# A three-product float32 gated expert layer: P1 copied into P2's bank and summed there by TensorE, the second prefix added into P5's bank

## The chip, the cores and the metric

The kernel runs on one core of one Trainium2 chip. The metric is the device time of one launch in microseconds (us); lower is better. Engines are named as in the profile: PE (TensorE's matmuls), PEld (its weight loads), DVE (VectorE), ACT (ScalarE), POOL (GpSimd), SP (SyncE, which issues the DMAs).

## The reference

```python
def _L0_cond_ref(h, gating_probs, shared_gate_prob, Wg, Wu, Wd, Sg, Su, Sd):   # h: 16 x 256 tokens x 256
    g = jnp.einsum('bsd,edf->ebsf', h, Wg)                                       # 8 experts, f = 1024
    u = jnp.einsum('bsd,edf->ebsf', h, Wu)
    expert_outs = jnp.einsum('ebsf,efd->ebsd', jax.nn.silu(g) * u, Wd)
    expert_output = jnp.einsum('be,ebsd->bsd', gating_probs, expert_outs)
    shared = jnp.einsum('bsf,fd->bsd', jax.nn.silu(h @ Sg) * (h @ Su), Sd)
    sg = shared_gate_prob[:, :, None]
    return (1.0 - sg) * expert_output + sg * shared
x = x + _L0_cond_ref(x, ...)
```

All of it is float32. The shared weights are a ninth expert whose coefficient is the shared gate.

## The kernel before

**Tiling.** The 4096 tokens are 8 tiles of 512 columns, taken in 4 groups of two (t = 0 and 1). For each group the kernel goes through 9 experts, and in each through 8 chunks of 128 of the 1024 inner features. One (group, expert, chunk) is a *unit*, numbered n; there are 4 x 9 x 8 = 288. Expert 0 of a group is written out; experts 1 to 8 are a hardware loop of 8 units, so there are 32 loop iterations.

**A unit.** Gate and up of one chunk for both tiles are a 2 x 2 by 2 x 2 block product, made Strassen-Winograd fashion from seven 128 x 128 by 128 x 512 products P1 to P7 instead of eight, plus four products into the down projection (two for each tile). Each product is three matmuls (`product`): a number is split in a high part (hi, rounded to fp32r) and a rest (lo), and hi·hi, hi·lo and lo·hi are summed. That is 11 products or 33 matmuls in a unit. The prefix sums are U2 = P1 + P6 and U3 = U2 + P7, kept in the bank `chain_ps` (two of them, by the parity of n); then gate of tile 0 = P1 + P2, gate of tile 1 = U2 + P5 + P3, up of tile 1 = U3 + P5, and up of tile 0 = U3 + P4.

**What the engines do in a unit.** PE issues P4 of the unit before (P4(n-1)), then P1, P5, the two down products of tile 0 for unit n-2, P6, P2, P3, P7, and the two down products of tile 1 for unit n-1. ACT copies P1 and P5 and, after P6, U2 to SBUF ("taps", L411, L414, L421), applies Silu twice (L429, L432), makes the hi parts of h of both tiles (L395 for tile 1, L400 for tile 0) and the hi part of the weights of unit n+2 in two casts (L374). DVE makes gate0 = tap of P1 + P2 (L516), gate1 = tap of U2 + (P5 + P3) (L522), up1 = tap of P5 + U3 (L528, into the bank of P2), then h1 = silu x coefficient x up1 in place (L493, two halves), the lo of h1 (L508), h0 in place in the chain's bank (L482, two halves) and the lo of h0 (L501). POOL makes the sums and the lo parts of the weights and of x. The trace joins names that differ in a digit: `p_up_ps` is the bank `p2_up1_ps`, `p_ps` is `p53_ps`, `tap_p` is tap_p1 or tap_p5, `h_hi` is h0_hi or h1_hi.

**What sets the order.** It is written out by hand. Every engine executes its own queue in order, and engines wait for each other through semaphores (`wait_ge`); `after(engine, signal, count)` is such a wait that is left out in the first units. The units are software-pipelined: ACT's and DVE's unit n begins with the second half of the work on unit n-1:

```python
h1_hi_of(n - 1)      # ACT, then the tap of P1(n), the tap of P5(n), h0_hi_of(n - 1), the weights' first cast
...
h1_lo_of(n - 1)      # DVE, then h0, h0_lo_of(n - 1), gate0(n), gate1(n), up_of_1(n), h1(n)
```

In the first six units of groups 0 to 2 ACT also casts forms of the next group's x (`x_form_hi`, L390; one in each of five units, two in the sixth), between the second weight cast and the first Silu. In the first two units of groups 1 to 3 DVE adds the down banks of the group before into `acc` (L534), behind h1.

Of the kernel before, what the change touches and what calls it, by code (L numbers as in the profile page):

```python
# [25 lines left out]
def moe_kernel(nc, xT, w, probs, shared_gate, out):  # L26
# [12 lines left out]
    with ExitStack() as ctx:  # L39
# [229 lines left out]
        def _(pe):  # L269
# [16 lines left out]
            def down0(k, start, stop, each=False):  # L286
                for c in range(DC):
                    last = product(
                        down_ps[:, 0, c, :], k % SLOTS, D0 + c, h0_hi[:, k % 2, :], h0_lo[:, k % 2, :], start, stop
                    )  # L290
                    if each and c == 0:
                        last.then_inc(down_done[0], 1)
                last.then_inc(down_done[0], 1)

            def down1(k, start, stop):
                for c in range(DC):
                    last = product(down_ps[:, 1, c, :], k % SLOTS, D0 + c, h1_hi[:], h1_lo[:], start, stop)
                last.then_inc(down_done[1], 1)
# [9 lines left out]
            def unit(g, e, k):  # L308
# [37 lines left out]
                if not isinstance(n, int) or n > 0:  # L346
                    pe.wait_ge(h_lo_done[1], n)
                    opens = in_first and k == 1
                    if opens:
                        after(pe, added[1], g)  # L350
                    down1((k - 1) % CHUNKS, start=opens, stop=first)
# [334 lines left out]
```

## Time and profile before

| | |
|---|---|
| median of 3 runs | 2179.14 us (2177.81 to 2179.55) |
| the profiled execution's own time | 2178.35 us |
| its span, from the first to the last instruction | 2176.5 us |
| granted TensorE clock, mean | 1.000 |
| PE busy | 2159.4 us, 9504 matmuls |
| DVE busy | 1490.3 us, 2623 instructions |
| ACT busy | 1532.3 us, 2623 instructions |
| POOL busy | 1386.7 us, 2046 instructions |

A profile's page gives busy times, groups of instructions with the idle time ahead of them and who ended it, and the chain of work that ended last; the timeline lists instructions by start. One matmul shows as 0.39 us long, but they overlap: the next one starts before the first has ended. An ACT or DVE instruction, too, may start before the end of the one before it on its engine.

### The profile page before, as it was taken

What the parts mean: (1) busy time and instruction counts of PE and PEld (TensorE: products, weight loads), DVE (VectorE), ACT (ScalarE), POOL (GpSimd) and SP (SyncE); (2) the same over time, 40 slices, a digit from 0 to 9 for tenths busy, and PEclk for the clock granted to TensorE, in tenths of its full rate; (3) what the DMA queues carried; (4) which work ended last, traced back from release to release, by engine and by line L of the source; (5) the groups of instructions that cost most, each with busy time, mean ns of one, the idle gap of its engine ahead of it and who ended that gap; (6) DMA issues with size and microseconds to landing.
All of it is one profiled execution on the core that took longest, in us unless ns stands there. A gap on an engine that the chain in (4) does not pass through costs nothing.

```text
span 2176.5 us, 34574 instructions
## 1 busy us (share of the span) xinstructions
PE 2159.4 (99%) x9504; PEld 1785.0 (82%) x9504; DVE 1490.3 (68%) x2623; ACT 1532.3 (70%) x2623; POOL 1386.7 (64%) x2046
## 2 busy tenths in 40 slices
PE   7999999999999999999999999999999999999999
PEld 5888888888888888888888888888888888888887
DVE  6666666666766666666676666666667666666666
ACT  7767776776777677767777776777677677767775
POOL 7766666666866666666686666666666666666663
PEclk9999999999999999999999999999999999999999
DMA  4111111111211111111121111111112111111110
GB/s 151 59 51 56 52 51 51 58 51 51 72 57 51 51 57 51 51 51 58 51 71 54 55 51 51 58 51 51 51 58 70 52 54 54 51 51 58 51 51 27
DMA packets 44683, 122.22 MB, mean 56 GB/s; under 512 B 5088, under 2 KB 5344, under 8 KB 44640
## 3 DMA queue, kind: packets, MB, share of 16 engines
q1 hardware_dynamic: 44640, 121.73, 18.0%
q8 instruction: 17, 0.28, 0.1%
q14 instruction: 26, 0.21, 0.0%
HBM read 117.51 MB, written 4.19 MB: 56 GB/s over the span
## 4 chain that ended last, share of the span: by engine, by line
PE 99%; DMA 0%; SPq 0%; POOL 0%; DVE 0%; ACT 0%; issue 0%; DVEq 0%; ACTq 0%
PE chain_ps L274 12%; PE down_ps L274 12%; PE down_ps L275 12%; PE down_ps L276 12%; PE chain_ps L275 12%; PE chain_ps L276 12%; PE p_ps L275 6%; PE p_ps L274 6%; PE p_ps L276 6%; PE p_up_ps L275 3%; PE p_up_ps L274 3%; PE p_up_ps L276 3%; DMA acc<-xT 0%; POOL w_lo L205 0%; SPq L145 0%
## 5 line engine op out<-in xcount | busy, mean ns | idle before, releaser
L205 POOL TENSOR_TENSOR w_lo<-w_raw,w_hi 128x384 fp32r<-128x384 f32 x861 | 850.8, 1019 | 731.5 <-ACT w_hi L374 731.5
L190 POOL TENSOR_TENSOR w_raw<-w_raw 128x128 f32<-128x128 f32 x1148 | 506.9, 464 | 32.6 <-DMA w_raw<-w 10.1
L274 PE MATMUL chain_ps<-x_hi,w_hi 128*128 128x512 f32 x1152 | 449.4, 390 | 11.7 <-DVE w_lo L590 5.8
L275 PE MATMUL chain_ps<-x_lo,w_hi 128*128 128x512 f32 x1152 | 448.6, 389 | 0.0
L276 PE MATMUL chain_ps<-x_hi,w_lo 128*128 128x512 f32 x1152 | 448.6, 389 | 0.0
L274 PE MATMUL down_ps<-h_hi,w_hi 128*128 128x512 f32 x1152 | 448.2, 389 | 0.2 <-DVE h_lo L508 0.2
L275 PE MATMUL down_ps<-h_lo,w_hi 128*128 128x512 f32 x1152 | 448.1, 389 | 0.0
L276 PE MATMUL down_ps<-h_hi,w_lo 128*128 128x512 f32 x1152 | 448.1, 389 | 0.0
L374 ACT CAST w_hi<-w_raw 128x768 fp32r<-128x768 f32 (+1 forms) x574 | 387.3, 675 | 85.1 <-PE down_ps L276 78.8
L395 ACT CAST h_hi<-p_up_ps 128x512 fp32r<-128x512 f32 x288 | 169.0, 587 | 307.8 <-DVE p_up_ps L493 307.8
L516 DVE TENSOR_TENSOR gate<-tap_p,p_up_ps 128x512 f32<-128x512 f32 x288 | 198.0, 687 | 251.0 <-PE p_up_ps L276 251.0
L501 DVE TENSOR_TENSOR h_lo<-chain_ps,h_hi 128x512 fp32r<-128x512 f32 x288 | 199.2, 692 | 200.8 <-ACT h_hi L400 175.5
L508 DVE TENSOR_TENSOR h_lo<-p_up_ps,h_hi 128x512 fp32r<-128x512 f32 x288 | 199.3, 692 | 188.7 <-ACT h_hi L395 188.7
L493 DVE SCALAR_TENSOR_TENSOR p_up_ps<-silu,coef,p_up_ps 128x256 f32<-128x256 f32 x576 | 253.7, 487 | 36.2 <-DVE p_up_ps L528 7.9
L274 PEld LDWEIGHTS chain_ps<-x_hi,w_hi 128*128 128x128 f32 x1152 | 216.4, 188 | 58.9 <-DVE w_lo L590 5.8
L274 PEld LDWEIGHTS down_ps<-h_hi,w_hi 128*128 128x128 f32 x1152 | 216.2, 188 | 45.6 <-DVE h_lo L508 0.6
L276 PEld LDWEIGHTS chain_ps<-x_hi,w_lo 128*128 128x128 f32 x1152 | 216.5, 188 | 45.0
L275 PEld LDWEIGHTS chain_ps<-x_lo,w_hi 128*128 128x128 f32 x1152 | 216.5, 188 | 44.6
L276 PEld LDWEIGHTS down_ps<-h_hi,w_lo 128*128 128x128 f32 x1152 | 216.2, 188 | 44.9
L275 PEld LDWEIGHTS down_ps<-h_lo,w_hi 128*128 128x128 f32 x1152 | 216.2, 188 | 44.8
L482 DVE SCALAR_TENSOR_TENSOR chain_ps<-silu,coef,chain_ps 128x256 f32<-128x256 f32 x576 | 251.1, 482 | 0.4 <-PE chain_ps L276 0.4
L411 ACT COPY tap_p<-chain_ps 128x512 f32<-128x512 f32 x288 | 169.6, 589 | 111.1 <-PE chain_ps L276 111.0
(47 smaller groups left out, 2852.6 us busy)
## 6 DMA issues: line engine op xcount, KB each, us to landing
w_raw<-w SPq DMA_DIRECT2D x287, 384.0 KB, 3.0
outT<-acc SPq DMA_DIRECT2D x7, 512.0 KB, 4.4
acc<-xT SPq DMA_DIRECT2D x6, 512.0 KB, 9.4
acc<-xT SPq DMA_DIRECT2D x4, 256.0 KB, 4.7
outT<-acc SPq DMA_DIRECT2D x2, 256.0 KB, 2.8
w_raw<-w SPq DMA_DIRECT2D x1, 256.0 KB, 3.0
w_raw<-w SPq DMA_DIRECT2D x1, 128.0 KB, 5.2
probs_sb<-probs SPq DMA_DIRECT2D x1, 64.0 KB, 7.7
```

The source lines that it names most:

```text
L190: nc.gpsimd.tensor_tensor(raw[:, cols(dst, dst)], raw[:, cols(a, a)], raw[:, cols(b, b)], op).then_inc(w_sums, 1)
L205: ins = nc.gpsimd.tensor_tensor(w_lo[:, s, c], w_raw[:, s, c], w_hi[:, s, c].bitcast(F32), ALU.subtract)
L274: nc.tensor.matmul(bank, w_hi[:, s, c], hi, start=start, stop=False, **on)
L275: nc.tensor.matmul(bank, w_hi[:, s, c], lo, start=False, stop=False, **on)
L276: return nc.tensor.matmul(bank, w_lo[:, s, c], hi, start=False, stop=stop, **on)
L374: nc.scalar.copy(w_hi[:, s, c], w_raw[:, s, c]).then_inc(w_hi_done, 1)
L411: nc.scalar.copy(tap_p1[:], chain_ps[:, k % 2, :]).then_inc(p1_tapped, 1)
L482: ins = nc.vector.scalar_tensor_tensor(sums, silu[:, 0, s], coef_of(g, e, 0, half), sums, ALU.mult, ALU.mult)
L493: ins = nc.vector.scalar_tensor_tensor(p2_up1_ps[:, s], silu[:, 1, s], coef_of(g, e, 1, half), p2_up1_ps[:, s], ALU.mult, ALU.mult)
L501: nc.vector.tensor_tensor(h0_lo[:, k % 2], chain_ps[:, k % 2, :], h0_hi[:, k % 2].bitcast(F32), ALU.subtract).then_inc(h_lo_done[0], 1)
L508: nc.vector.tensor_tensor(h1_lo[:], p2_up1_ps[:], h1_hi[:].bitcast(F32), ALU.subtract).then_inc(h_lo_done[1], 1)
L516: nc.vector.tensor_tensor(gate[:, 0], tap_p1[:], p2_up1_ps[:], ALU.add).then_inc(gate0_done, 1)
```

## The change

DVE's two gate additions become one addition of another kind, and of ACT's three copies to SBUF one goes and one goes to PSUM:

- P1 is copied by ACT (the *seed*) not to SBUF but into the bank that P2 will go to, now called `y_ps`, and P2 is accumulated on top of it by PE. gate0 is then in the bank without an addition. One matmul at the start opens the bank.
- U4 = tap of P5 + U2 is added by DVE (`u4`) into P5's own bank, now called `z_ps`, and P3 is accumulated on top. gate1 is then in that bank. The tap of U2 is gone.
- Both Silus read a PSUM bank.
- PE's order becomes P4(n-1), P1, P5, first down product of tile 0, P6, second down product of tile 0, P2, P7, P3, and the two of tile 1. P6 waits for the seed, P7 for u4.
- The seed waits for the lo of h1 of the unit before (`h_lo_done[1]`), since it overwrites h1's bank. It is ahead of the cast of h0 on ACT, as the tap of P1 was; the lo of h1 is ahead of h0 on DVE, as before.
- On ACT the second weight cast and x's forms now stand behind the first Silu and ahead of the second.

```diff
-        tap_p1 = sb("tap_p1", [P, TOKENS])
...
-        tap_u2 = sb("tap_u2", [P, TOKENS])
-        gate = sb("gate", [P, 2, TOKENS])
...
                 if opening:
                     first_w(0)
+                    nc.tensor.matmul(y_ps[:], w_hi[:, 0, 0:P], x_of(0, B11, True)[0], start=True, stop=True).then_inc(
+                        y_opened, 1
+                    )
...
-                after(pe, gate1_done, n)
+                after(pe, silu_done[1], n)
...
-                pe.wait_ge(p1_tapped, n + 1)
+                product(z_ps[:], s, S1, *x_of(g, T1, first), start=True, stop=True).then_inc(p5_done, 1)
+                down0_part(0)
+                pe.wait_ge(p1_seeded, n + 1)
                 product(chain, s, S2, *x_of(g, T2, first), start=False, stop=True, goes_on=True).then_inc(p6_done, 1)
-                after(pe, h_lo_done[1], n)
-                product(p2_up1_ps[:], s, A12, *x_of(g, B21, first), start=True, stop=True).then_inc(p2_done, 1)
-                pe.wait_ge(p5_tapped, n + 1)
-                product(p53_ps[:], s, S4, *x_of(g, B22, first), start=False, stop=True, goes_on=True).then_inc(p3_done, 1)
-                pe.wait_ge(u2_tapped, n + 1)
+                down0_part(1)
+                product(y_ps[:], s, A12, *x_of(g, B21, first), start=False, stop=True, goes_on=True).then_inc(p2_done, 1)
+                pe.wait_ge(u4_done, n + 1)
...
                 product(chain, s, S3, *x_of(g, T3, first), start=False, stop=True, goes_on=True).then_inc(p7_done, 1)
...
+                product(z_ps[:], s, S4, *x_of(g, B22, first), start=False, stop=True, goes_on=True).then_inc(p3_done, 1)
+                down1_both()
...
                 act.wait_ge(p1_done, n + 1)
-                after(act, gate0_done, n)
-                nc.scalar.copy(tap_p1[:], chain_ps[:, k % 2, :]).then_inc(p1_tapped, 1)
+                if first:
+                    act.wait_ge(y_opened, 1)
+                after(act, h_lo_done[1], n)
+                nc.scalar.copy(y_ps[:], chain_ps[:, k % 2, :]).then_inc(p1_seeded, 1)
...
-                act.wait_ge(p6_done, n + 1)
-                after(act, gate1_done, n)
-                nc.scalar.copy(tap_u2[:], chain_ps[:, k % 2, :]).then_inc(u2_tapped, 1)
+                act.wait_ge(p2_done, n + 1)
+                after(act, h0_done, n)
+                nc.scalar.activation(silu[:, 0], y_ps[:], ACT.Silu).then_inc(silu_done[0], 1)
                 if ahead:
                     weight_hi(n + AHEAD, (k + AHEAD) % SLOTS, 1)
...
-                nc.scalar.activation(silu[:, 1], gate[:, 1], ACT.Silu).then_inc(silu_done[1], 1)
+                nc.scalar.activation(silu[:, 1], z_ps[:], ACT.Silu).then_inc(silu_done[1], 1)
...
+            def u4(n, k):
+                dve.wait_ge(p6_done, n + 1)
+                dve.wait_ge(p5_tapped, n + 1)
+                nc.vector.tensor_tensor(z_ps[:], tap_p5[:], chain_ps[:, k % 2, :], ALU.add).then_inc(u4_done, 1)
...
-                gate0(n)
-                gate1(n)
+                u4(n, k)
                 up_of_1(n, k)
```

On PE, the first matmul of every product of one steady unit, before; `p53_ps` is P5's and P3's bank, `p2_up1_ps` P2's:

```order
L274 MATMUL chain_ps<-x_hi,w_hi 128x512 [waits h0_lo_done,w_lo_done]
...
L274 MATMUL p53_ps<-x_hi,w_hi 128x512 [waits gate1_done]
...
L274 MATMUL down_ps<-h0_hi,w_hi 128x512 [waits h0_lo_done]
...
L274 MATMUL down_ps<-h0_hi,w_hi 128x512
...
L274 MATMUL chain_ps<-x_hi,w_hi 128x512 [waits p1_tapped]
...
L274 MATMUL p2_up1_ps<-x_hi,w_hi 128x512 [waits h1_lo_done]
...
L274 MATMUL p53_ps<-x_hi,w_hi 128x512 [waits p5_tapped]
...
L274 MATMUL chain_ps<-x_hi,w_hi 128x512 [waits u2_tapped]
```

and now; `gate0_up1_ps` is `y_ps`, `p5_gate1_ps` is `z_ps`:

```order
L270 MATMUL chain_ps<-x_hi,w_hi 128x512 [waits h0_lo_done,w_lo_done]
...
L270 MATMUL p5_gate1_ps<-x_hi,w_hi 128x512 [waits silu1_done]
...
L270 MATMUL down_ps<-h0_hi,w_hi 128x512 [waits h0_lo_done]
...
L270 MATMUL chain_ps<-x_hi,w_hi 128x512 [waits p1_seeded]
...
L270 MATMUL down_ps<-h0_hi,w_hi 128x512
...
L270 MATMUL gate0_up1_ps<-x_hi,w_hi 128x512
...
L270 MATMUL chain_ps<-x_hi,w_hi 128x512 [waits u4_done]
...
L270 MATMUL p5_gate1_ps<-x_hi,w_hi 128x512
```

P6 stands one product earlier, and P7, which waits for DVE's u4, stands one product earlier and ahead of P3.

On ACT, one steady unit before, from the cast of h1 to the second Silu:

```order
L395 CAST h1_hi<-p2_up1_ps 128x512 [waits down1_done,h1_done]
L411 COPY tap_p1<-chain_ps 128x512 [waits gate0_done,p1_done]
L414 COPY tap_p5<-p53_ps 128x512 [waits up1_done,p5_done]
L400 CAST h0_hi<-chain_ps 128x512 [waits down0_done,h0_done]
L374 CAST w_hi<-w_raw 128x768 [waits down0_done,w_sums]
L421 COPY tap_u2<-chain_ps 128x512 [waits gate1_done,p6_done]
L374 CAST w_hi<-w_raw 128x384 [waits down0_done,w_sums]
L429 ACTIVATE silu<-gate 128x512 [waits h0_done,gate0_done]
L432 ACTIVATE silu<-gate 128x512 [waits h1_done,gate1_done]
```

and now:

```order
L402 CAST h1_hi<-gate0_up1_ps 128x512 [waits down1_done,h1_done]
L420 COPY gate0_up1_ps<-chain_ps 128x512 [waits h1_lo_done,p1_done]
L423 COPY tap_p5<-p5_gate1_ps 128x512 [waits up1_done,p5_done]
L407 CAST h0_hi<-chain_ps 128x512 [waits down0_done,h0_done]
L381 CAST w_hi<-w_raw 128x768 [waits down0_done,w_sums]
L430 ACTIVATE silu<-gate0_up1_ps 128x512 [waits h0_done,p2_done]
L381 CAST w_hi<-w_raw 128x384 [waits down0_done,w_sums]
L438 ACTIVATE silu<-p5_gate1_ps 128x512 [waits h1_done,p3_done]
```

One copy fewer, and the copy of P1 waits for DVE's lo of h1 as well.

On DVE, one steady unit now, from the lo of h1 to h1; before, L516 and L522 stood where u4 (L521) stands now:

```order
L514 TENSOR_TENSOR h1_lo<-gate0_up1_ps,h1_hi 128x512 [waits down1_done,h1_hi_done]
L488 SCALAR_TENSOR_TENSOR chain_ps<-silu,coef,chain_ps 128x256 [waits silu0_done,p4_done]
L488 SCALAR_TENSOR_TENSOR chain_ps<-silu,coef,chain_ps 128x256
L507 TENSOR_TENSOR h0_lo<-chain_ps,h0_hi 128x512 [waits down0_done,h0_hi_done]
L521 TENSOR_TENSOR p5_gate1_ps<-tap_p5,chain_ps 128x512 [waits p5_tapped,p6_done]
L526 TENSOR_TENSOR gate0_up1_ps<-tap_p5,chain_ps 128x512 [waits silu0_done,p7_done]
L499 SCALAR_TENSOR_TENSOR gate0_up1_ps<-silu,coef,gate0_up1_ps 128x256 [waits up1_done,silu1_done]
```

## Rows read from the trace of the kernel before

**Rows 1.** The page: engines' busy time, then PE's costliest group with idle and releaser.

```profile
PE 2159.4 (99%) x9504; PEld 1785.0 (82%) x9504; DVE 1490.3 (68%) x2623; ACT 1532.3 (70%) x2623; POOL 1386.7 (64%) x2046
...
L274 PE MATMUL chain_ps<-x_hi,w_hi 128*128 128x512 f32 x1152 | 449.4, 390 | 11.7 <-DVE w_lo L590 5.8
```

**Rows 2.** Timeline of PE, steady unit: start, length in us, instruction.

```profile
999.87 0.39 PE L274 MATMUL chain_ps<-x_hi,w_hi 128*128 128x512 f32 x1
...
1003.04 0.39 PE L276 MATMUL down_ps<-h_hi,w_lo 128*128 128x512 f32 x1
...
1004.63 0.39 PE L274 MATMUL p_ps<-x_hi,w_hi 128*128 128x512 f32 x1
...
1007.35 0.39 PE L274 MATMUL chain_ps<-x_hi,w_hi 128*128 128x512 f32 x1
```

**Rows 3.** Timeline of DVE, the same unit and the next.

```profile
1005.51 0.69 DVE L522 TENSOR_TENSOR gate<-tap_u,p_ps 128x512 f32<-128x512 f32 x1
...
1006.99 0.88 DVE L493 SCALAR_TENSOR_TENSOR p_up_ps<-silu,coef,p_up_ps 128x256 f32<-128x256 f32 x2
1008.52 0.69 DVE L508 TENSOR_TENSOR h_lo<-p_up_ps,h_hi 128x512 fp32r<-128x512 f32 x1 [0.65 <-ACT h_hi L395]
1009.13 0.87 DVE L482 SCALAR_TENSOR_TENSOR chain_ps<-silu,coef,chain_ps 128x256 f32<-128x256 f32 x2
1010.69 0.69 DVE L501 TENSOR_TENSOR h_lo<-chain_ps,h_hi 128x512 fp32r<-128x512 f32 x1 [0.69 <-ACT h_hi L400]
```

**Rows 4.** Timeline of ACT, the same stretch.

```profile
1003.52 0.83 ACT L374 CAST w_hi<-w_raw 128x768 fp32r<-128x768 f32 x1 [0.34 <-PE down_ps L276]
1004.26 0.58 ACT L421 COPY tap_u<-chain_ps 128x512 f32<-128x512 f32 x1
...
1007.90 0.59 ACT L395 CAST h_hi<-p_up_ps 128x512 fp32r<-128x512 f32 x1 [1.04 <-DVE p_up_ps L493]
...
1009.59 0.59 ACT L414 COPY tap_p<-p_ps 128x512 f32<-128x512 f32 x1
1010.07 0.59 ACT L400 CAST h_hi<-chain_ps 128x512 fp32r<-128x512 f32 x1
```

**Rows 5.** By line: ACT's casts of x by source, min/median/max ns.

```profile
L390 ACT CAST x_hi<-acc x12: 617/622/626, 3.4 to 1124.8; 128x512 fp32r<-128x512 f32 x12
...
L390 ACT CAST x_hi<-down_ps x4: 585/586/588, 6.8 to 11.1; 128x512 fp32r<-128x512 f32 x4
```

**Rows 6.** Timeline of the opening: PE waits for an addition of DVE's.

```profile
18.40 0.70 DVE L528 TENSOR_TENSOR p_up_ps<-tap_p,chain_ps 128x512 f32<-128x512 f32 x1
...
19.15 0.50 PE L274 MATMUL chain_ps<-x_hi,w_hi 128*128 128x512 f32 x1 [0.79 <-DVE p_up_ps L528]
...
19.49 0.40 PE L275 MATMUL chain_ps<-x_lo,w_hi 128*128 128x512 f32 x1
```

**Rows 7.** Timeline of ACT, then of DVE, where a new expert's loop iteration begins.

```profile
671.38 0.59 ACT L395 CAST h_hi<-p_up_ps 128x512 fp32r<-128x512 f32 x1 [1.12 <-DVE p_up_ps L493]
...
672.08 0.69 DVE L508 TENSOR_TENSOR h_lo<-p_up_ps,h_hi 128x512 fp32r<-128x512 f32 x1 [0.81 <-ACT h_hi L395]
```

**Rows 8.** Timeline of ACT with a form of x, and of DVE around an addition to acc.

```profile
555.94 0.51 ACT L374 CAST w_hi<-w_raw 128x384 fp32r<-128x384 f32 x1
556.35 0.62 ACT L390 CAST x_hi<-acc 128x512 fp32r<-128x512 f32 x1
556.87 0.63 ACT L429 ACTIVATE silu<-gate 128x512 f32<-128x512 f32 x1
...
558.19 0.88 DVE L493 SCALAR_TENSOR_TENSOR p_up_ps<-silu,coef,p_up_ps 128x256 f32<-128x256 f32 x2
...
560.11 0.68 DVE L508 TENSOR_TENSOR h_lo<-p_up_ps,h_hi 128x512 fp32r<-128x512 f32 x1
```

**Rows 9.** Timeline of PE in the opening.

```profile
14.39 0.63 PE L275 MATMUL chain_ps<-x_lo,w_hi 128*128 128x512 f32 x1
14.82 0.63 PE L276 MATMUL chain_ps<-x_hi,w_lo 128*128 128x512 f32 x1
```

More of the change, by code:

```diff
@@ L284, in x_of, with down0, down1 @@
                 return x_hi[:, g % 2, form, :], x_lo[:, g % 2, form, :]
[L286 to L298, printed above, removed]
+            def down0(k, c, start, stop, each=False):
+                last = product(
+                    down_ps[:, 0, c, :], k % SLOTS, D0 + c, h0_hi[:, k % 2, :], h0_lo[:, k % 2, :], start, stop
+                )
+                if c == DC - 1 or each:
+                    last.then_inc(down_done[0], 1)
+            def down1(k, c, start, stop):
+                last = product(down_ps[:, 1, c, :], k % SLOTS, D0 + c, h1_hi[:], h1_lo[:], start, stop)
+                if c == DC - 1:
+                    last.then_inc(down_done[1], 1)
             def p4(g, k, n, first=False):
@@ L318, in unit, with down0_part, down1_both @@
                     p4(g - 1 if first else g, (k - 1) % CHUNKS, n - 1, first=in_first and k == 1)
+                def down0_part(c):
+                    if not isinstance(n, int) or n > 1:
+                        opens = in_first and k == 2
+                        if c == 0:
+                            pe.wait_ge(h_lo_done[0], n - 1)
+                            if opens:
+                                after(pe, added[0], g)
+                        down0((k - 2) % CHUNKS, c, start=opens, stop=in_first and k == 1)
+                def down1_both():
+                    if not isinstance(n, int) or n > 0:
+                        pe.wait_ge(h_lo_done[1], n)
+                        opens = in_first and k == 1
+                        if opens:
+                            after(pe, added[1], g)
+                        for c in range(DC):
+                            down1((k - 1) % CHUNKS, c, start=opens, stop=first)
                 if opening:
                     first_w(0)
+                    nc.tensor.matmul(y_ps[:], w_hi[:, 0, 0:P], x_of(0, B11, True)[0], start=True, stop=True).then_inc(
+                        y_opened, 1
+                    )
                 else:
@@ L345, in unit @@
                 product(chain, s, S3, *x_of(g, T3, first), start=False, stop=True, goes_on=True).then_inc(p7_done, 1)
[L346 to L351, printed above, removed]
+                product(z_ps[:], s, S4, *x_of(g, B22, first), start=False, stop=True, goes_on=True).then_inc(p3_done, 1)
+                down1_both()
             for g in range(GROUPS):
@@ L360, in _ @@
             pe.wait_ge(h_lo_done[0], LAST)
-            down0(CHUNKS - 2, start=False, stop=False)
+            for c in range(DC):
+                down0(CHUNKS - 2, c, start=False, stop=False)
             pe.wait_ge(h_lo_done[1], LAST + 1)
-            down1(CHUNKS - 1, start=False, stop=True)
+            for c in range(DC):
+                down1(CHUNKS - 1, c, start=False, stop=True)
             pe.wait_ge(h_lo_done[0], LAST + 1)
-            down0(CHUNKS - 1, start=False, stop=True, each=True)
+            for c in range(DC):
+                down0(CHUNKS - 1, c, start=False, stop=True, each=True)
         @block.scalar
@@ L394, in h1_hi_of @@
                 after(act, down_done[1], n)
-                nc.scalar.copy(h1_hi[:], p2_up1_ps[:]).then_inc(h_hi_done[1], 1)
+                nc.scalar.copy(h1_hi[:], y_ps[:]).then_inc(h_hi_done[1], 1)
             def h0_hi_of(n, k):
@@ L426, in unit @@
                         x_form_hi(g + 1, form)
-                act.wait_ge(gate0_done, n + 1)
-                after(act, h0_done, n)
-                nc.scalar.activation(silu[:, 0], gate[:, 0], ACT.Silu).then_inc(silu_done[0], 1)
-                act.wait_ge(gate1_done, n + 1)
+                act.wait_ge(p3_done, n + 1)
                 after(act, h1_done, n)
-                nc.scalar.activation(silu[:, 1], gate[:, 1], ACT.Silu).then_inc(silu_done[1], 1)
+                nc.scalar.activation(silu[:, 1], z_ps[:], ACT.Silu).then_inc(silu_done[1], 1)
             act.wait_ge(warm_set, 1)
@@ L507, in h1_lo_of @@
                 after(dve, down_done[1], n)
[L508 removed]
+                nc.vector.tensor_tensor(h1_lo[:], y_ps[:], h1_hi[:].bitcast(F32), ALU.subtract).then_inc(
                     h_lo_done[1], 1
                 )
[L512 to L522 removed]
+            def u4(n, k):
+                dve.wait_ge(p6_done, n + 1)
+                dve.wait_ge(p5_tapped, n + 1)
+                nc.vector.tensor_tensor(z_ps[:], tap_p5[:], chain_ps[:, k % 2, :], ALU.add).then_inc(u4_done, 1)
             def up_of_1(n, k):
                 dve.wait_ge(p7_done, n + 1)
[L526 to L528 removed]
+                dve.wait_ge(silu_done[0], n + 1)
+                nc.vector.tensor_tensor(y_ps[:], tap_p5[:], chain_ps[:, k % 2, :], ALU.add).then_inc(up1_done, 1)
             def add(g, t, n):
```

36 lines of the change are left out of this document (7 added, 29 removed).

## The prediction

> **What bounds the kernel now.** I read the page first, then the timeline of one steady unit engine by engine. PE is busy for 2159.4 of 2176.5 us, and the idle time ahead of its costliest group is 11.7 us in all, 5.8 of it in one wait on the opening's weights [rows 1]. In the steady part PE does not wait: from one P4 to the next it takes 1007.35 − 999.87 = 7.48 us [rows 2], which is 33 matmuls at 0.227 us or 11 products at 0.68. 288 units at 7.48 are 2154 us. Neither kernel differs in matmuls (the change adds one), so the change cannot take much from the time; the question is whether DVE and ACT still hand PE each bank in time. The reader should see in the timelines that they are in a loop with PE, but that this loop has slack before.
>
> **How late each hand-over is now.** I follow one chain around: P3(n) → Silu of gate1 → h1 → its hi → its lo → seed of n+1 → tap of P5 → hi of h0 → lo of h0 → u4 → P7 → P3(n+1). It is a closed chain only after the change. The seed overwrites the bank of h1, so it waits for the lo of h1; the tap of P5 and the hi of h0 stand behind the seed on ACT; u4 stands behind the lo of h0 on DVE; and P7 waits for u4 ahead of P3. If the sum around it is over 7.48, each unit takes that sum.
>
> - P3's first matmul to the reader of its bank: 1005.51 − 1004.63 = 0.88 [rows 2, 3].
> - Silu of gate1, now from PSUM: 0.63 from SBUF [rows 8]. ACT's casts of x take 622 ns from SBUF and 586 from PSUM [rows 5], so I take 0.036 off: 0.60. Ends for the range: 0.63 and 0.60. To h1's start 0.03, the gap by which 1007.90 follows the end of h1 at 1006.99 + 0.88 [rows 3, 4].
> - h1, hi, and on to the start of the lo of h1: 1008.52 − 1006.99 = 1.53 [rows 3], with hi in between at 1007.90 [rows 4].
> - Lo of h1 0.69 [rows 3], then the seed's start. The seed waits for two signals (P1 and the lo). Where ACT had such a second wait that came last, the weight cast after the down product, the gap was 1003.52 − (1003.04 + 0.39) = 0.09 [rows 2, 4], so 0.09 and not 0.03. Together 0.78.
> - Seed to tap of P5: no copy from PSUM to PSUM stands in the trace. I take ACT's pitch between the tap of P5 and the hi of h0, 1010.07 − 1009.59 = 0.48 [rows 4]. Ends: 0.44, if the destination saves as much as the source does [rows 5], and 0.59, the copy's whole length.
> - Tap of P5 to the start of the lo of h0: 1010.69 − 1009.59 = 1.10 [rows 3, 4]. h0 itself does not hold this up: it starts 0.61 after the lo of h1 and takes 0.87 [rows 3], done 1.48 after that start, while the hi of h0 is due on ACT only 0.78 + 0.48 + 0.48 = 1.74 after it.
> - Lo of h0 to u4, DVE's pitch: 1009.13 − 1008.52 = 0.61 [rows 3]. u4's other inputs are there by then: P6 starts 2.72 after the unit's P4, so is done at 3.60, and u4 starts at about 3.97.
> - u4 is of the form of L528, from whose start to PE's release 19.15 − 18.40 = 0.75 passed [rows 6]. PE then starts with the weight load: the second matmul came at 19.49, 0.34 later in place of 0.227, so 0.11 is lost on top [rows 6].
> - P7's three matmuls ahead of P3: 0.68.
>
> Sum: 0.88 + 0.60 + 0.03 + 1.53 + 0.78 + 0.48 + 1.10 + 0.61 + 0.75 + 0.11 + 0.68 = 7.55. Of the roundings (two decimals in each row) I take 7.555. Against 7.48 that is 0.075 us late at P7 in every unit.
>
> The Trainium skill, "Perfetto Trace Analysis", section "Optimizing Scalar/DVE Operations", gives ScalarE's access overhead as about 93 ns on SBUF and 51 on PSUM. The trace agrees as to the source (622 against 586); that a destination saves as much no row shows. If it does, with the sum as it stands, the chain is 7.51 and the time some 11 us lower.
>
> **The sum.**
>
> - Steady lateness: 287 × 0.075 = 21.5 us.
> - At the start of a loop iteration the waits have dynamic counts. The hi of h1 came 1.12 after the tap ahead of it and not 1.04 [rows 4, 7], 0.08 more; the lo of h1 came 672.08 − 671.38 = 0.70 after its hi, not 0.62 [rows 3, 4, 7], 0.08 more; the lo of h0 waits in the same form, taken as 0.09 more. These lay in slack before and are all in the chain now: 32 iterations × 0.25 = 8.0 us.
> - x's forms stand between the second weight cast and the Silu of gate1. The first weight cast waits for the second down product (starts at 3.40 in the unit, so 3.40 + 0.45 + 0.39 + 0.09 = 4.33), the Silu of gate0 follows 0.74 later (the pitch 1004.26 − 1003.52 [rows 4]) at 5.07, the second weight cast about 0.50 later, then 0.41 to a form and 0.52 for each form [rows 8]: 5.07 + 0.50 + 0.41 + 0.52 = 6.50, where P3 allows 5.44 + 0.075 + 0.88 = 6.40. One form is 0.10 late, two 0.62: 3 × (5 × 0.10 + 0.62) = 3.4 us. Without a form the cast is through at 5.98 and costs nothing.
> - The additions to acc: with one between, the lo of h1 starts 560.11 − 558.19 = 1.92 after h1 [rows 8], not 1.53: 6 × 0.39 = 2.3 us.
> - What costs nothing. P6 stands one product earlier (starts at 2.72) and waits for the seed: the seed starts at 1.78 in the unit, ends at 2.37, releases PE at 2.42 and with the 0.11 at 2.53, 0.19 ahead. The missing gate additions (0.69 each) and the tap of U2 (0.58) leave engines that are 68% and 70% busy [rows 1]. up1 can start at about 5.8 (P7 done, first Silu done), ends at 6.5, and P4 needs it at 7.48. The one more matmul of the opening, and its wait on ACT, lie before a P1 that waits on x and weights anyway: within 0.5 us.
>
> Total: 21.5 + 8.0 + 3.4 + 2.3 = 35.2 us. Against the profiled execution's own 2178.35 us (span 2176.5 and 1.85 around it) that gives 2213.6; the median of the runs is 0.8 us above that execution. I predict 2214 us, 1.6% slower.
>
> **The rivals.**
>
> *A: the chain is longer than I think.* If the seed holds ACT for its whole 0.59 and Silu stays at 0.63, the chain is 7.555 + 0.11 + 0.03 = 7.695, another 287 × 0.14 = 40 us: 2254. For it: nothing in the trace writes PSUM from ACT. Against: every pitch of two ACT instructions that nothing holds is well below the first one's length [rows 4]. 8%.
>
> *B: the steady chain just fits.* At 7.48 or a little under, only the loop starts, forms and additions cost: 14 us at exactly 7.48, about 8 with 0.1 us of slack. 2186 to 2192. It needs both PSUM savings and 0.04 more off my sum. 9%.
>
> *C: no difference.* It takes slack of about 0.2 us, so a chain of 7.3, for instance if ACT started the hi of h0 ahead of the seed (the order shows that it does not). 2179. 4%.
>
> *D: faster, by the opening.* PE's waits on the opening are 11.7 us [rows 1]. 5.8 of them are on weights that the change does not touch, which leaves 5.9. If the steady chain fits with 0.2 of slack and nearly all of those 5.9 go, because P4 no longer waits for a gate addition and a tap, the time is 2173. It decides from 4.4 us on. Of single waits in those 5.9 the row shown is 0.79 [rows 6]. 3%.
>
> *E: the granted clock falls.* In the opening at the lower level (1.2 GHz) matmuls came 14.82 − 14.39 = 0.43 apart [rows 9], against 0.227 at 2.4 GHz; it is granted in full with the opening's gaps of about a microsecond behind it. If the regular gaps at P7 brought it down for a twentieth of the matmuls, 475 × 0.20 = 95 us come on top: 2309. 2%. The Trainium skill, "TensorE: Matmul & The Clock Gate", section "A second HAM failure mode: psum-queue depth-cycling", tells of a kernel whose clock went up and down by such small idle gaps; there is no such fall in this trace, and the new gap is 1% of a unit.
>
> **How the numbers follow.** My forecast, a steady stall of 0.03 to 0.12 us, has 74%, and its own range is 2198 to 2228: 0.60 or 0.63 for the Silu is 9 us, 0.44 or 0.48 for the seed's pitch 11, rounding of eleven terms a few. The range 2186 to 2238 takes in B and leaves out C, D, A and E, 17%, and the ends of my own case, about 2%. The measurement tells 0.2% (4.4 us) from no change. Slower by more than that are my forecast, A, B and E: 93%; same C: 4%; faster D: 3%.
>
> **What would show it.** In the profile of the changed kernel PE's idle time should stand ahead of P7's first matmul (a `chain_ps` row) with DVE's u4 as releaser, some 280 times, and a unit should take 7.55 to 7.56, 7.8 at a loop start. Busy PE stays about 2160 or shows the longer first matmul of P7 (0.50). ACT's seed should start 1.78 after P4, u4 at 3.97; the Silus should take 0.60; the seed to tap pitch tells A from my case. The granted clock should stay at 1.000. The prediction is wrong if PE shows no wait on u4, if the seed starts by P1's end (1.55) rather than the lo of h1, or if P6 waits for it.

## The result

The changed kernel takes 2225.68 us (median of 4 runs, 2225.38 to 2225.81), the one before 2178.89 us (4 runs, 2177.81 to 2179.55). The ratio is 1.0214, with a 95% interval of 1.0202 to 1.0227: slower by 46.8 us. 2214 was forecast, with a range of 2186 to 2238.

The page of the changed kernel, engines' busy time and the costliest group of PE, as in [rows 1]:

```profile
span 2223.8 us, 33419 instructions
...
PE 2205.4 (99%) x9505; PEld 1762.3 (79%) x9505; DVE 1272.2 (57%) x2335; ACT 1306.0 (59%) x2335; POOL 1385.5 (62%) x2046
...
PE 97%; DVE 1%; ACT 1%; issue 1%; DMA 0%; POOL 0%; SPq 0%; DVEq 0%; ACTq 0%
...
L270 PE MATMUL chain_ps<-x_hi,w_hi 128*128 128x512 f32 x1152 | 475.5, 413 | 7.5 <-ACT gate_up_ps L420 5.8
...
L270 PEld LDWEIGHTS chain_ps<-x_hi,w_hi 128*128 128x128 f32 x1152 | 216.1, 188 | 126.7 <-DVE p_gate_ps L521 79.0
```

and the weight loads of the same group in the page of the kernel before:

```profile
L274 PEld LDWEIGHTS chain_ps<-x_hi,w_hi 128*128 128x128 f32 x1152 | 216.4, 188 | 58.9 <-DVE w_lo L590 5.8
```

DVE and ACT lost 218 and 226 us of work and the kernel is slower, so neither was the bound. PE still reads 99% busy, its own idle column shows only 7.5 us, and the chain that ended last (the row that begins with PE 97%) is put down to PE for 97%: none of the three shows that DVE and ACT hold PE up in every unit. The loss shows in two other numbers: the mean of this group's matmuls went from 390 to 413 ns (P7's first matmul, which waits for its weights, shows as 0.50 us long and not as idle), and the weight loads ahead of them stood 126.7 us idle instead of 58.9, 79.0 of it ended by u4 (L521). Neither number is the loss itself: 23 ns on 1152 matmuls are 26 us, and a weight load that is in time comes well ahead of its matmul, so its idle time counts more than PE loses. The loss is read from the distance of one unit to the next.

Two units of PE, the first two behind the start of a loop iteration, from the second down product of tile 0:

```profile
1003.78 0.39 PE L272 MATMUL gate_up_ps<-x_hi,w_lo 128*128 128x512 f32 x1
1004.09 0.50 PE L270 MATMUL chain_ps<-x_hi,w_hi 128*128 128x512 f32 x1
1004.43 0.40 PE L271 MATMUL chain_ps<-x_lo,w_hi 128*128 128x512 f32 x1
1004.67 0.40 PE L272 MATMUL chain_ps<-x_hi,w_lo 128*128 128x512 f32 x1
1004.90 0.40 PE L270 MATMUL p_gate_ps<-x_hi,w_hi 128*128 128x512 f32 x1
...
1011.51 0.39 PE L272 MATMUL gate_up_ps<-x_hi,w_lo 128*128 128x512 f32 x1
...
1012.02 0.39 PE L271 MATMUL chain_ps<-x_lo,w_hi 128*128 128x512 f32 x1
...
1012.49 0.40 PE L270 MATMUL p_gate_ps<-x_hi,w_hi 128*128 128x512 f32 x1
```

P7's second matmul is at 1004.43, 0.65 after the last one of P2, where two steps of 0.227 would be 0.45. So P7 is 0.20 late there, and 1012.02 − 1011.51 − 0.45 = 0.06 in the next unit; in the medians of the later units of an iteration it is 0.06 to 0.08, and the rest of the 0.10 that a unit loses is in the matmuls behind the stall, which come 0.23 to 0.24 apart for a while. From P3 to P3 it is 1012.49 − 1004.90 = 7.59 us, against 7.48 in [rows 2].

ACT in the same stretch:

```profile
1004.81 0.50 ACT L381 CAST w_hi<-w_raw 128x384 fp32r<-128x384 f32 x1
1005.79 0.60 ACT L438 ACTIVATE silu<-p_gate_ps 128x512 f32<-128x512 f32 x1 [0.48 <-PE p_gate_ps L272]
1007.34 0.59 ACT L402 CAST h_hi<-gate_up_ps 128x512 fp32r<-128x512 f32 x1 [0.95 <-DVE gate_up_ps L499]
1008.74 0.57 ACT L420 COPY gate_up_ps<-chain_ps 128x512 f32<-128x512 f32 x1 [0.81 <-DVE h_lo L514]
1009.22 0.60 ACT L423 COPY tap_p<-p_gate_ps 128x512 f32<-128x512 f32 x1
1009.70 0.60 ACT L407 CAST h_hi<-chain_ps 128x512 fp32r<-128x512 f32 x1
```

and DVE:

```profile
1006.42 0.88 DVE L499 SCALAR_TENSOR_TENSOR gate_up_ps<-silu,coef,gate_up_ps 128x256 f32<-128x256 f32 x2 [0.63 <-ACT silu L438]
1007.96 0.69 DVE L514 TENSOR_TENSOR h_lo<-gate_up_ps,h_hi 128x512 fp32r<-128x512 f32 x1 [0.66 <-ACT h_hi L402]
...
1010.34 0.69 DVE L507 TENSOR_TENSOR h_lo<-chain_ps,h_hi 128x512 fp32r<-128x512 f32 x1 [0.90 <-ACT h_hi L407]
1010.95 0.69 DVE L521 TENSOR_TENSOR p_gate_ps<-tap_p,chain_ps 128x512 f32<-128x512 f32 x1
```

Here is the whole chain: P3 1004.90, Silu 1005.79, h1 1006.42, its hi 1007.34, its lo 1007.96, seed 1008.74, tap of P5 1009.22, hi of h0 1009.70, lo of h0 1010.34, u4 1010.95, P7's second matmul 1012.02, P3 1012.49. Where a row shows a wait, the wait names the link before; the tap of P5, the hi of h0 and u4 show none, and start at ACT's and DVE's pitch (0.48, 0.48 and 0.61) behind the instruction ahead of them.

### The profile page after: what moved, and what is told of

Read it like the earlier page. It is cut to its first block, busy times and chain, and to the rows that moved or that the text cites. A ratio compares the mean times of both kernels' runs of the same rounds, so it can differ in the third digit from the quotient of the medians.

```text
span 2223.8 us, 33419 instructions
## 1 busy us (share of the span) xinstructions
PE 2205.4 (99%) x9505; PEld 1762.3 (79%) x9505; DVE 1272.2 (57%) x2335; ACT 1306.0 (59%) x2335; POOL 1385.5 (62%) x2046
## 4 chain that ended last, share of the span: by engine, by line
PE 97%; DVE 1%; ACT 1%; issue 1%; DMA 0%; POOL 0%; SPq 0%; DVEq 0%; ACTq 0%
PE chain_ps L270 13%; PE chain_ps L271 12%; PE chain_ps L272 12%; PE down_ps L270 11%; PE down_ps L272 11%; PE down_ps L271 11%; PE p_gate_ps L270 6%; PE p_gate_ps L272 6%; PE p_gate_ps L271 6%; PE gate_up_ps L270 3%; PE gate_up_ps L271 3%; PE gate_up_ps L272 3%; DVE h_lo L514 0%; DMA w_raw<-w 0%; DVE gate_up_ps L499 0%
## 5 line engine op out<-in xcount | busy, mean ns | idle before, releaser
L270 PE MATMUL chain_ps<-x_hi,w_hi 128*128 128x512 f32 x1152 | 475.5, 413 | 7.5 <-ACT gate_up_ps L420 5.8
L526 DVE TENSOR_TENSOR gate_up_ps<-tap_p,chain_ps 128x512 f32<-128x512 f32 x288 | 200.5, 696 | 314.0 <-PE chain_ps L272 305.5
L499 DVE SCALAR_TENSOR_TENSOR gate_up_ps<-silu,coef,gate_up_ps 128x256 f32<-128x256 f32 x576 | 253.6, 486 | 176.4 <-ACT silu L438 176.4
L402 ACT CAST h_hi<-gate_up_ps 128x512 fp32r<-128x512 f32 x288 | 169.1, 587 | 279.9 <-DVE gate_up_ps L499 279.9
L270 PEld LDWEIGHTS chain_ps<-x_hi,w_hi 128*128 128x128 f32 x1152 | 216.1, 188 | 126.7 <-DVE p_gate_ps L521 79.0
L514 DVE TENSOR_TENSOR h_lo<-gate_up_ps,h_hi 128x512 fp32r<-128x512 f32 x288 | 199.4, 692 | 188.8 <-ACT h_hi L402 188.8
L420 ACT COPY gate_up_ps<-chain_ps 128x512 f32<-128x512 f32 x288 | 164.2, 570 | 238.9 <-DVE h_lo L514 238.9
```

Source lines behind the costliest of these rows:

```text
L270: nc.tensor.matmul(bank, w_hi[:, s, c], hi, start=start, stop=False, **on)
L402: nc.scalar.copy(h1_hi[:], y_ps[:]).then_inc(h_hi_done[1], 1)
L499: ins = nc.vector.scalar_tensor_tensor(y_ps[:, s], silu[:, 1, s], coef_of(g, e, 1, half), y_ps[:, s], ALU.mult, ALU.mult)
L514: nc.vector.tensor_tensor(h1_lo[:], y_ps[:], h1_hi[:].bitcast(F32), ALU.subtract).then_inc(h_lo_done[1], 1)
L526: nc.vector.tensor_tensor(y_ps[:], tap_p5[:], chain_ps[:, k % 2, :], ALU.add).then_inc(up1_done, 1)
```

## The experiments

All are edits of the changed kernel. Theory: the closed chain sets the unit's time. The rivals named in the expectations are that P7 is late only by its place in PE's order (P), that PE itself is slower on banks that other engines wrote (M), and that it is the load on ACT.

**Two kernels with the same extra work.** A copy of 128x512 from one half of a spare tile to the other is added to every unit on ACT, once on the chain and once off it. The comments in the cut say which kernel has which line.

```diff
                 nc.scalar.copy(y_ps[:], chain_ps[:, k % 2, :]).then_inc(p1_seeded, 1)
+                if not first:
+                    nc.scalar.copy(spare[:, 1], spare[:, 0])     # e12: ahead of the tap of P5
...
                 if not first:
                     h0_hi_of(n - 1, k - 1)
+                    nc.scalar.copy(spare[:, 1], spare[:, 0])     # e13: behind the hi of h0
```

> The changed kernel with one more ACT copy in each unit (128x512, SBUF to SBUF, between two halves of a spare tile), between the seed and the tap of P5. Theory (closed chain): ACT's pitch for such a copy was 0.52 us and lies in the chain in full, so the steady unit goes from 7.58 to 8.10, and the time by 286 x 0.52 = 149 us to about 2375. Rival (what costs is the load on ACT or PSUM, or PE's place of P7): between 2225 and 2300, and the same as with the copy elsewhere.

> The changed kernel with the same spare copy behind the hi of h0 on ACT, ahead of the weights' first cast, where ACT sat idle for 0.88 us. It is the same load on ACT, but off the chain. Theory: no change, 2225 to 2227. Rival (load on ACT): as slow as with the copy between the seed and the tap of P5.

On the chain: 2373.62 us (2 runs), ratio to before 1.0893 (1.0861 to 1.0924), 147.9 us over the changed kernel where 149 were expected. Off the chain: 2225.98 us, ratio 1.0215 (1.0185 to 1.0245), 0.3 us over it. ACT's timeline with the copy on the chain:

```profile
1000.90 0.59 ACT L404 CAST h_hi<-gate_up_ps 128x512 fp32r<-128x512 f32 x1 [1.08 <-DVE gate_up_ps L504]
1002.30 0.57 ACT L422 COPY gate_up_ps<-chain_ps 128x512 f32<-128x512 f32 x1 [0.81 <-DVE h_lo L519]
1002.79 0.62 ACT L424 COPY spare<-spare 128x512 f32<-128x512 f32 x1
1003.31 0.59 ACT L427 COPY tap_p<-p_gate_ps 128x512 f32<-128x512 f32 x1
...
1009.01 0.59 ACT L404 CAST h_hi<-gate_up_ps 128x512 fp32r<-128x512 f32 x1 [0.95 <-DVE gate_up_ps L504]
```

The copy costs its pitch, 1003.31 − 1002.79 = 0.52, not its length of 0.62, and the unit is 1009.01 − 1000.90 = 8.11 us long. The same load elsewhere costs nothing (2225.98 against 2225.68 us): it is not ACT's load, it is the place.

**The first down product of tile 1 between P2 and P7.** u4 gets 0.68 us more.

```diff
+                down1_part(0)
                 pe.wait_ge(u4_done, n + 1)
                 product(chain, s, S3, *x_of(g, T3, first), start=False, stop=True, goes_on=True).then_inc(p7_done, 1)
                 product(z_ps[:], s, S4, *x_of(g, B22, first), start=False, stop=True, goes_on=True).then_inc(p3_done, 1)
-                down1_both()
+                down1_part(1)
```

> The changed kernel with the first down product of tile 1 between P2 and P7, so that u4 has 0.68 us more. Rival P (P7 is late by its place): the stall of 0.10 in each unit goes, 2179 to 2185. Theory (closed chain): P3 is 0.68 later as well, so the seed of the next unit comes 0.68 later against P6, and the loop closes by seed, P6, four products and P3: 0.88 + 0.63 + 0.92 + 0.62 + 0.78 + 0.73 + 2.72 + 0.68 = 7.96 us for each unit. That is 0.48 over 7.48 in 286 units, 137 us, and some 14 of loop starts, forms and additions: about 2330.

2336.93 us (2 runs), ratio 1.0725 (1.0702 to 1.0748), 7 more than the 2330 expected, and a steady unit takes 8.00 us for the 7.96 expected: P, which had 2179 to 2185, is out. What PE waited for:

```profile
PE chain_ps L270 <- ACT gate_up_ps L421: 75.4, 288, 4.0
PE gate_up_ps L334 <- DVE w_lo L588: 5.8, 1, 5.8
```

The wait has moved, in all 288 units, from u4 at P7 to the seed at P6, and u4 ends the wait of a weight load 2 times instead of 288. A later P3 gives this loop no slack, it only closes the loop elsewhere.

**The seed behind the cast of h0**, the order that the change avoids.

```diff
                 if not first:
+                    h0_hi_of(n - 1, k - 1)
                 ...
                 nc.scalar.copy(y_ps[:], chain_ps[:, k % 2, :]).then_inc(p1_seeded, 1)
                 ...
-                if not first:
-                    h0_hi_of(n - 1, k - 1)
```

> The changed kernel with the cast of h0 ahead of the seed on ACT, the order that the change avoids. Theory: the seed then waits for h0 too and comes 1.99 us after the start of the lo of h1 instead of 0.78, and the loop closes by P6: 3.05 + 2.00 + 0.73 + 2.74 = 8.52 us a unit, 1.04 over 7.48, about 297 us and 16 of the rest: about 2490, with PE's idle time ahead of P6 and none ahead of P7. Rival (P7 is late by its place and by DVE's order): u4 could come earlier, 2225 or less.

2506.44 us (2 runs), ratio 1.1503 (1.1482 to 1.1524). PE's waits:

```profile
PE chain_ps L270 <- ACT gate_up_ps L422: 243.7, 288, 4.4
```

The time is 16 us over the 2490 expected: a steady unit takes 8.56 to 8.58 us, where the loop by P6 was reckoned at 8.52, and in all 288 units PE waits for the seed at P6. So the seed's place ahead of the cast is the better of the two, and still on a chain that is too long.

**u4 ahead of the lo of h0 on DVE.**

```diff
-                    h0_lo_of(n - 1, k - 1)
                 u4(n, k)
+                if before[0] >= 0:
+                    h0_lo_of(n - 1, k - 1)
```

> The changed kernel with u4 ahead of the lo of h0 on DVE. Theory: u4 is held up by the lo of h0, which its result does not need. Ahead of it, it waits for P6 alone (done 3.60 us after P4), and what is left of the chain goes by seed, P6 and three products to P7, 7.28 us in all. It fits in 7.48 with 0.2 of slack, so all but the largest delays vanish: about 2181 to 2183. Rival M (PE slower on those banks): 2225, for PE does the same work on the same banks. Rival: the lo of h0, now later, stops a down product or P1 in its turn: 2190 or more.

2183.71 us (10 runs, 2183.18 to 2185.09), ratio 1.0022 (1.0012 to 1.0031), just over the 2181 to 2183 expected: 42 of the 46.8 us are gone, with the same banks, the same matmuls and the same waits. M is out. DVE's timeline:

```profile
1003.56 0.69 DVE L514 TENSOR_TENSOR h_lo<-gate_up_ps,h_hi 128x512 fp32r<-128x512 f32 x1 [0.65 <-ACT h_hi L402]
1004.17 0.87 DVE L488 SCALAR_TENSOR_TENSOR chain_ps<-silu,coef,chain_ps 128x256 f32<-128x256 f32 x2
1006.16 0.69 DVE L521 TENSOR_TENSOR p_gate_ps<-tap_p,chain_ps 128x512 f32<-128x512 f32 x1 [1.12 <-PE chain_ps L272]
1006.76 0.68 DVE L507 TENSOR_TENSOR h_lo<-chain_ps,h_hi 128x512 fp32r<-128x512 f32 x1
```

u4 now waits for PE's P6 and not for ACT's hi of h0, and the lo of h0, which could start 0.64 behind its hi (at 1005.30 in ACT's timeline of this run, so at 1005.94) and starts 0.82 later, stops nobody.

**The hi of h0 ahead of the tap of P5 on ACT**, another way to shorten the chain.

```diff
+                if not first:
+                    h0_hi_of(n - 1, k - 1)
                 act.wait_ge(p5_done, n + 1)
                 after(act, up1_done, n)
                 nc.scalar.copy(tap_p5[:], z_ps[:]).then_inc(p5_tapped, 1)
-                if not first:
-                    h0_hi_of(n - 1, k - 1)
```

> The changed kernel with ACT's hi of h0 ahead of the tap of P5. Theory: the hi of h0 then waits for h0 itself, due 1.51 us after the start of the lo of h1 instead of 1.74, so the chain is about 7.35 us and fits in 7.48; only the loop starts (32 x 0.12), the additions to acc and the double forms of x still cost: about 2186. Rival M: 2225. Rival P: the tap of P5 is 0.5 later and u4 waits for it, so it could be slower than 2225.

2190.91 us (4 runs), ratio 1.0056 (1.0038 to 1.0074), 5 more than expected. The steady unit is 7.48, as expected; in the unit at a loop start the median from P4 to P4 is 7.66 and in the next 7.52, so 0.22 for each of 32 iterations, not 0.12. That is 3 of the 5.

**The seed's waits written the other way round**: the lo of h1 first, then P1.

```diff
-                act.wait_ge(p1_done, n + 1)
                 ...
                 after(act, h_lo_done[1], n)
+                act.wait_ge(p1_done, n + 1)
```

> The changed kernel with the seed's two waits written the other way round: the lo of h1 first, then P1. Nothing else differs. Theory (closed chain P3, Silu, h1, its hi, its lo, seed, tap of P5, hi of h0, lo of h0, u4, P7, P3 sets the unit's time): the leg from the lo of h1 to the seed, 0.78 us, loses the 0.05 to 0.06 that a second wait adds when it is the last to come, so the steady unit goes from 7.58 to 7.53 and the time from 2225.7 to about 2210. Rival P (P7 is late by its place in PE's order only): the seed is early enough anyway, P7's lateness comes from the tap of P5 and stays, 2225. Rival M (PE itself is slower on banks that ACT or DVE wrote): 2225.

2219.56 us (4 runs), ratio 1.0186 (1.0168 to 1.0204): 6 us gained, not 15. The leg itself shrank as expected, in the median of all units from 0.780 to 0.725 us. ACT's timeline shows where the rest went:

```profile
1005.92 0.57 ACT L420 COPY gate_up_ps<-chain_ps 128x512 f32<-128x512 f32 x1 [0.76 <-DVE h_lo L514]
1006.43 0.59 ACT L423 COPY tap_p<-p_gate_ps 128x512 f32<-128x512 f32 x1
```

The tap of P5 now comes 0.51 behind the seed, not 0.48. P5's second matmul started at 1005.78 in that trace, so its first at 1005.55, and 0.88 later P5 can be read, at 1006.43. With the seed earlier, the tap waits for P5 itself: in most units it starts 0.426 behind the start of P5's third matmul, the same delay as from P3's third matmul to the Silu. The chain from P5 to P7 is 0.88 + 0.48 + 0.625 + 0.61 + 0.85 = 3.445 in the medians of this run, against 3.40 for PE's five products, so it is about 0.045 too long on its own. I had not looked for this second floor.

**Half of the change: u4 alone**, with gate0 as an addition on DVE from a tap of P1 in SBUF. The first Silu then reads gate0 from SBUF; the diff leaves out that line and the new tiles.

```diff
-                product(y_ps[:], s, A12, *x_of(g, B21, first), start=False, stop=True, goes_on=True).then_inc(p2_done, 1)
+                after(pe, h_lo_done[1], n)
+                product(y_ps[:], s, A12, *x_of(g, B21, first), start=True, stop=True).then_inc(p2_done, 1)
...
-                after(act, h_lo_done[1], n)
-                nc.scalar.copy(y_ps[:], chain_ps[:, k % 2, :]).then_inc(p1_seeded, 1)
+                after(act, gate0_done, n)
+                nc.scalar.copy(tap_p1[:], chain_ps[:, k % 2, :]).then_inc(p1_seeded, 1)
...
                 u4(n, k)
+                gate0(n)
```

> Half of the change: U4 goes into P5's bank and P3 is summed on it, with the new order on PE; gate0 stays an addition on DVE from a tap of P1 in SBUF, so there is no seed and no wait for the lo of h1 ahead of it. Theory: the chain is now open, for nothing in it waits for the unit before; but u4 is still behind the lo of h0, and that goes back to the tap of P5, which can't start before P5 is done at 2.24 us. From there 0.48 + 0.64 + 0.61 + 0.85 = 2.58 gives 4.82, against P7's place at 4.76: about 0.055 late in each unit. That is 16 us, and 3 for the lo of h0 at loop starts: about 2197. Rival (only the seed's closed chain costs): 2179. Rival M (PE slower on banks written by DVE): some 2202, half of the loss or more, with no stall shown at P7.

2220.63 us (4 runs), ratio 1.0193 (1.0177 to 1.0208), 23 more than expected. On ACT:

```profile
1002.59 0.64 ACT L428 ACTIVATE silu<-gate_sb 128x512 f32<-128x512 f32 x1 [0.52 <-DVE gate_sb L525]
1003.12 0.50 ACT L381 CAST w_hi<-w_raw 128x384 fp32r<-128x384 f32 x1
1003.53 0.59 ACT L436 ACTIVATE silu<-p_gate_ps 128x512 f32<-128x512 f32 x1
...
1006.69 0.59 ACT L421 COPY tap_p<-p_gate_ps 128x512 f32<-128x512 f32 x1
1007.20 0.59 ACT L407 CAST h_hi<-chain_ps 128x512 fp32r<-128x512 f32 x1
```

and on DVE, the addition to gate0 and h0:

```profile
1001.86 0.69 DVE L525 TENSOR_TENSOR gate_sb<-tap_p,gate_up_ps 128x512 f32<-128x512 f32 x1 [0.32 <-PE gate_up_ps L274]
...
1006.29 0.87 DVE L486 SCALAR_TENSOR_TENSOR chain_ps<-silu,coef,chain_ps 128x256 f32<-128x256 f32 x2
```

I had called the chain open. It is not: the addition to gate0 holds up the first Silu (0.52 us idle, ended by L525), the weight cast and the second Silu follow it without a gap, and so h1, its lo and h0 come late as well. The hi of h0 follows the tap by 0.51: h0, started at 1006.29 and 0.87 long, is through at 1007.16. So it waits for h0, and the loop closes over two units: from P2 by the addition, both Silus, h1 and h0 with their parts, and u4 to P7 of the next unit it is 8.30 us in the median, and from there to P2 of the unit after 6.82 on PE, together 15.12 for two units, or 7.56 each. A steady unit is 7.57, and one at a loop start 7.87. The lateness per unit, 0.086 for the 0.055 expected, is 9 of the 23 us; the loop starts took 10 us for 3, and the rest is in the first units of the groups.

**The other half: the seed alone**, with gate1 as an addition on DVE from a tap of U2, which stands ahead of the weights' first cast, and P3 ahead of P7. The second Silu then reads gate1 from SBUF; the diff shows PE's and DVE's lines alone.

```diff
-                pe.wait_ge(u4_done, n + 1)
+                pe.wait_ge(p5_tapped, n + 1)
+                product(z_ps[:], s, S4, *x_of(g, B22, first), start=False, stop=True, goes_on=True).then_inc(p3_done, 1)
+                pe.wait_ge(u2_tapped, n + 1)
...
                 product(chain, s, S3, *x_of(g, T3, first), start=False, stop=True, goes_on=True).then_inc(p7_done, 1)
-                product(z_ps[:], s, S4, *x_of(g, B22, first), start=False, stop=True, goes_on=True).then_inc(p3_done, 1)
...
-                u4(n, k)
+                gate1(n)
```

> The other half: P1 is seeded into P2's bank and P2 summed on it; gate1 stays an addition on DVE from a tap of U2 (made ahead of the weights' first cast), and PE does P3 ahead of P7 as before. The seed still waits for the lo of h1. Theory: no u4, so P7 does not wait for the lo of h0. The seed reaches P6 with 0.13 us of slack, so the steady unit stays 7.48, and only loop starts (0.03 each), the additions to acc and the forms cost: about 2181 to 2183. Rival (the seed itself is what costs, a copy from PSUM to PSUM or its wait): 2195 or more.

2198.06 us (4 runs), ratio 1.0088 (1.0072 to 1.0103), 16 more than expected. On DVE:

```profile
1000.59 0.69 DVE L529 TENSOR_TENSOR gate_sb<-tap_u,p_gate_ps 128x512 f32<-128x512 f32 x1 [1.41 <-PE p_gate_ps L275]
1001.27 0.69 DVE L534 TENSOR_TENSOR gate_up_ps<-tap_p,chain_ps 128x512 f32<-128x512 f32 x1
1002.07 0.88 DVE L506 SCALAR_TENSOR_TENSOR gate_up_ps<-silu,coef,gate_up_ps 128x256 f32<-128x256 f32 x2
```

h1 waits for up1, not for the Silu, which I had left out; it puts the seed 0.1 later than I reckoned. From P3 by gate1, up1, h1 and the seed to P6 and on to P3 this chain is 0.02 too long: the medians of its legs sum to 7.50, the unit is 7.50, and the two units behind each loop start are 0.15 and 0.12 longer than 7.48. The halves alone cost 19 and 42 us, and together 47. So either half is enough for a loss, each by a loop of its own: with u4 alone nothing waits for the lo of h1 ahead of a copy, and 42 us are lost all the same. That the sum is less than the parts I put down to each half taking an addition out of the other's loop; no run shows that by itself.

**A version with what was learnt**: u4 ahead of the lo of h0, the lo of h1 as the seed's first wait, and x's forms behind the second Silu.

```diff
+                act.wait_ge(p3_done, n + 1)
+                after(act, h1_done, n)
+                nc.scalar.activation(silu[:, 1], z_ps[:], ACT.Silu).then_inc(silu_done[1], 1)
                 if new_x:
                     for form in X_AT.get(k, ()):
                         x_form_hi(g + 1, form)
-                act.wait_ge(p3_done, n + 1)
-                after(act, h1_done, n)
-                nc.scalar.activation(silu[:, 1], z_ps[:], ACT.Silu).then_inc(silu_done[1], 1)
```

The other two edits are those shown above.

> The changed kernel with u4 ahead of the lo of h0 on DVE, the lo of h1 as the seed's first-written wait, and x's forms behind the second Silu on ACT. Theory: u4 ahead gave 2183.7, with P6's wait for the seed as the nearest leg (7.30 us). The wait's order takes 0.05 off that leg and covers the loop starts, and the forms no longer delay the Silu: 2179.5 to 2181, as the kernel before. It cannot be much faster than before, since PE's 33 matmuls a unit are the floor: 288 x 7.48 = 2154 us plus the opening. Rival (some fixed loss lies in the new banks): 2183 or more, as without these two edits.

2180.32 us (11 runs), ratio 1.0007 (0.9998 to 1.0016), as expected: no difference from the kernel before, and 45 us under the change. The steady unit is 7.48 again, the time of PE's 33 matmuls, so little more is to be had while they stay. No version was found that beats the kernel before.

## Why the prediction was right, point by point

- **What bounds it, and the chain**: right, and not by luck: each link stands in the timelines above in the order given, a copy on it costs its full pitch and the same copy off it nothing, and a link taken off it gives back 42 us. The size was 12 us short of the measured 46.8.
- **The steady lateness**: 0.075 was forecast, 0.104 measured: the medians of the links over units 3 to 285 are 0.884, 0.632, 0.915, 0.620, 0.780, 0.482, 0.478, 0.638, 0.608, 0.851 and 0.694, in all 7.58. That is 30 us for 21.5. What was mis-sized is mostly two links. P7 to P3 takes 0.694 and not 0.68, because PE's matmuls come 0.23 to 0.24 apart behind the stall. Hi to lo of h0 takes 0.638 and not 0.62, since that cast is 606 ns long and not 592. From u4 to P7 it is 0.851 where 0.86 was taken, so a little of it cancels.
- **The choices between bounds**: the Silu from PSUM takes 0.598, 0.60 was taken. The pitch from the seed to the tap is 0.482, as the 0.48 of a copy to SBUF. The copy is shorter by its length alone, 570 ns against the 589 of the tap of P1 before. The Trainium skill, "ScalarE: Activation LUTs", section "Step-by-step: what each stage is for", says that ScalarE reaches PSUM faster than SBUF as a destination; the length agrees where ACT stood idle ahead of the copy, but ACT's next instruction starts no earlier for it, and directly behind the cast of h0 (the run with the seed behind it) the same copy is 592 ns long and the tap follows after 0.515. So the 0.48 holds for this place in the order and not for every one. The seed's second wait costs 0.055 (0.09 against 0.03 had been read off).
- **The loop starts**: 8.0 forecast. The three steps named cost 0.073, 0.089 and 0.088, which is 8.0. The first was read with the wrong name: in the kernel before, the instruction ahead of the hi of h1 is the second Silu and not a tap, and 1.12 and 1.04 are idle times behind it; from h1 to its hi it was 0.99 there instead of 0.91, so the 0.08 stands. A fourth was missed: in the unit behind it, h1 starts 0.127 later after its Silu. In the timeline of DVE of the changed kernel it is this row, against 0.63 in the steady one above:

```profile
693.61 0.88 DVE L499 SCALAR_TENSOR_TENSOR gate_up_ps<-silu,coef,gate_up_ps 128x256 f32<-128x256 f32 x2 [0.76 <-ACT silu L438]
```

  It is 4 us in all. Ahead of that h1 the trace has a register instruction of the same line (L499, at 693.49, 75 ns long) that also waits for the Silu; the coefficient's address comes from the loop's counter there. In the kernel before, h1 came 0.12 late there too, in slack.
- **Forms and additions**: 3.4 and 2.3 forecast, 2.1 and 2.3 measured. A double form costs 0.51 to 0.59 (0.62 was forecast). Of the five single ones of a group three cost nothing and two 0.06 to 0.10 (0.10 was forecast for each).
- **What costs nothing**: P6, up1 and the missing additions, right. The seed started 1.79 after P4 in the median, for 1.78, and P6 did not wait for it in a steady unit.
- **The sum**: 30 + 8 + 4 + 2 + 2 = 46, and 46.8 measured. Of the some 12 us that the forecast lacked 8.5 are the steady links and 4 the missed step at loop starts, less 1.3 at the forms.
- **What would show it**: here I was wrong. The wait is not in PE's idle column, which names u4 once; it is in the weight loads' (79.0 us, 288 times) and in the length of P7's first matmul. "Wrong if PE shows no wait on u4" would have misled whoever looked at PE's column alone.
- **Rivals**: A is out (pitch 0.482), B and C need slack that is not there, D is out, and E too: the granted clock stayed at 1.000. That record reads 1.00 in the opening as well, where [rows 9] has matmuls 0.43 apart, so the distances of the matmuls say more: in the changed kernel none but those at a wait is over 0.245.

## What to carry to other kernels

Before work is taken off engines that have time to spare, follow the new waits once around: a copy into a bank that the unit before still uses ties the units to each other, and then every link counts in full, by pitch, however idle its engine is. Such a tie need not be new, either: with u4 alone the loop closed through an addition and the Silus behind it. Delays that lay in slack before (loop starts, a rare extra instruction) are then paid, so leave some tenths of a microsecond in such a loop. What shortens it is the order within an engine: an instruction that another engine waits for goes ahead of one that nobody waits for yet, which here was worth 42 us for one line moved.
